# Expert blocks of a mixture-of-experts layer: two biases move from TensorE to VectorE

## The reference, cut to what matters

```python
logits = jnp.einsum('bsd,de->bse', input, Wg)          # E = 8 experts
top_vals, top_idx = jax.lax.top_k(softmax(logits), 2)  # two experts a token
h = relu(jnp.einsum('ebsd,edh->ebsh', xm, W1) + b1)    # 256 -> 512
y = jnp.einsum('ebsh,ehd->ebsd', h, W2) + b2           # 512 -> 256
out = jnp.sum(y * scores, axis=0)
```

## Time and profile before

| | |
|---|---|
| median of three runs | 1959.32 us |
| profiled execution, its own time | 1960.84 us |
| its span, first to last instruction | 1959.1 us |
| PE busy | 1750.1 us (89%) |
| DVE busy | 1140.5 us (58%) |
| ACT busy | 865.6 us (44%) |
| POOL busy | 1264.1 us (65%) |
| self-attention / cross-attention / experts (from the timeline) | to 217 / to 1698 / to 1959.1 us |

### The profile page before, as it was taken

How to read it: one execution, slowest core, us unless ns; L and a number is a source line. 1 busy time by engine, 2 the same in 40 slices (tenths; PEclk the granted TensorE clock), 3 DMA queues, 4 the chain that set the end, 5 groups by cost and what they waited for, 6 DMA issues and landing times. The chain is left out here.

```text
span 1959.1 us, 32737 instructions
## 1 busy us (share of the span) xinstructions
PE 1750.1 (89%) x10682; PEld 1225.8 (63%) x10682; DVE 1140.5 (58%) x2004; ACT 865.6 (44%) x1280; POOL 1264.1 (65%) x710
## 2 busy tenths in 40 slices
PE   6654799999989999998999999989999999648992
PEld 4544566676656666665666666656666665337991
DVE  4776455656565656656565656666665555563444
ACT  3223244444444544444444444544444444424443
POOL 3877247667677677686866766777668676236554
PEclk8776689999999999999999999999999999759996
DMA  6001300000200000010000000200000000032224
GB/s 193 1 22 34 117 1 23 1 22 0 77 1 23 22 2 23 0 55 22 22 1 24 1 22 0 77 1 23 22 1 23 16 0 1 33 123 77 70 71 140
DMA packets 38853, 68.09 MB, mean 35 GB/s; under 512 B 4600, under 2 KB 28544, under 8 KB 37696
## 3 DMA queue, kind: packets, MB, share of 16 engines
q1 hardware_dynamic: 34976, 56.12, 8.6%
q0 software_dynamic: 3744, 10.23, 1.7%
HBM read 52.84 MB, written 13.50 MB: 34 GB/s over the span
## 5 line engine op out<-in xcount | busy, mean ns | idle before, releaser
L1101 POOL TENSOR_TENSOR xa_total<-xa_total,xa_pexp 128x1024 f32<-128x1024 f32 (+1 forms) x341 | 832.3, 2441 | 62.0 <-ACT xa_pexp L1042 38.1
L1174 DVE TENSOR_REDUCE xa_parts<-ps_ring 128x1 f32<-128x402 f32 x1024 | 531.6, 566 | 269.8 <-PE ps_ring L987 256.4
L1042 ACT ACTIVATE xa_pexp<-ps_s 128x1024 f32<-128x1024 f32 (+1 forms) x416 | 426.5, 1027 | 397.6 <-PE ps_s L941 360.9
L955 PE MATMUL ps_pv<-xa_pexp,xa_v 128*64 128x512 f32 (+1 forms) x1664 | 398.7, 603 | 0.0
L955 PEld LDWEIGHTS ps_pv<-xa_pexp,xa_v 128*64 128x64 f32 (+1 forms) x1664 | 106.0, 136 | 182.1 <-issue 141.1
L941 PE MATMUL ps_s<-xa_q_neg,xa_row_one 64*128 64x512 f32 (+1 forms) x832 | 180.2, 391 | 0.0
L1101 POOL TENSOR_TENSOR xa_total<-xa_pexp 128x1024 f32<-128x1024 f32 x31 | 74.0, 2387 | 159.9 <-ACT xa_pexp L1042 158.6
L1077 ACT COPY xa_v<-ps_ring 128x256 f32<-128x256 f32 (+1 forms) x208 | 77.7, 374 | 204.1 <-PE ps_ring L926 202.2
L987 PE MATMUL ps_ring<-xa_k_hi,xa_q_hi 64*128 64x402 f32 x512 | 127.0, 377 | 6.0 <-DVE xa_parts L1174 5.0
L987 PE MATMUL ps_ring<-first_k_hi,xa_q_hi 64*128 64x402 f32 x512 | 123.8, 388 | 3.3 <-DVE xa_q_lo L1168 1.5
L1189 DVE RECIPROCAL xa_inv<-xa_sums 128x128 f32<-128x128 f32 x128 | 120.3, 942 | 2.9 <-ACT xa_sums L1064 2.7
(11 more groups left out here) (298 smaller groups left out, 3434.9 us busy)
## 6 DMA issues: line engine op xcount, KB each, us to landing
wa_raw<-in_pack_a SPq DMA_DIRECT2D x17, 768.0 KB, 4.5
ex_raw<-in_pack_e SPq DMA_DIRECT2D x8, 1024.0 KB, 5.9
ctx_raw<-in_ctxT SPq DMA_DIRECT2D x4, 1601.0 KB, 8.8
wb_raw<-in_pack_b SPq DMA_DIRECT2D x16, 256.0 KB, 2.7
ex_w_hi<-ybuf SPq DMA_DIRECT2D x8, 512.0 KB, 7.4
sa_xT<-in_xT SPq DMA_DIRECT2D x8, 256.0 KB, 6.3
X<-in_x SPq DMA_DIRECT2D x1, 2048.0 KB, 11.3
x_hi<-sa_x1s_hi SPq DMA_DIRECT2D x16, 128.0 KB, 2.1
```

The lines of the kernel that those rows point to most:

```text
L955: ins = nc.tensor.matmul(ps_pv[half(h), :], v[0:m, t, at:at + XD], pexp[0:m, buf, h, :], start=t == 0, stop=t == MT - 1)
L1042: nc.scalar.activation(pexp[0:m, buf], ps_s[0:m, (p * MT + t) % 2], ACT.Exp, scale=XD ** -0.5)\
L1101: engine.tensor_tensor(total[p][0:m], first, pexp[0:m, buf], ALU.add).then_inc(s["add_done"], 1)
L1174: nc.vector.tensor_reduce(parts[:, h, q, c:c + 1], ps_ring[:, r, 0:CW], AX.X, ALU.max)\
```

## The change

Both bias products leave PE. b1 and b2 are held as fp32 tables on all 128 partitions, and DVE adds the block's row while it moves h and y out of PSUM; the row is picked by a register that DVE loads itself. b2's table is loaded from DRAM by broadcast; b1, which lies turned in DRAM, is turned on PE at the start of the stage, copied to SBUF by DVE, stored to DRAM by SP and loaded again by broadcast; these stand ahead of the stores of `x2` in SP's list. ACT's `sel`, its copy of h and `bx` go. To make room (the tables take 24 KB a partition), xb, h_f, h_hi and h_lo have one buffer instead of two, the one-hot table `one_r` has half the size and is used in turn, and the routing's small tiles share their place with the block loop's. The second layer starts at the high part of h and waits for the low part only before its last four products. Cut to its core:

```diff
@@ Ahead.start
-        sp.dma_start(self.b2_raw[:], a["b2"]).then_inc(self.sems["small_in"], 16)
@@ experts, tiles
-        bx = sb("bx", [P, HID + E], F32R)
+        b1_all, b2_all = sb("b1_all", [P, NE, HID]), sb("b2_all", [P, NE, E])
-        xb_hi, xb_lo = sb("xb_hi", [P, 2, E], F32R), sb("xb_lo", [P, 2, E], F32R)
-        sel = sb("sel", [P, 2, P], F32R)
+        xb_hi, xb_lo = sb("xb_hi", [P, E], F32R), sb("xb_lo", [P, E], F32R)
+        h_f, h_hi, h_lo = sb("h_f", [P, HID]), sb("h_hi", [P, HID], F32R), sb("h_lo", [P, HID], F32R)
@@ sync
+            sp.dma_start(b2_all[:].rearrange("p e n -> p (e n)"),
+                         a["b2"].rearrange("(o e) n -> o (e n)", o=1).broadcast_to([P, NE * E])).then_inc(s["b2_in"], 16)
+            sp.wait_ge(s["b1_turned"], 1)
+            sp.dma_start(ahead.b1_rows.rearrange("o (e n) -> (o e) n", e=NE), b1_row[:]).then_inc(s["b1_out"], 16)
+            sp.wait_ge(s["b1_out"], 16)
+            sp.dma_start(b1_all[:].rearrange("p e n -> p (e n)"), ahead.b1_rows.broadcast_to([P, NE * HID]))\
+                .then_inc(s["b1_in"], 16)
             for b in range(B):
                 sp.wait_ge(s["x_done"], NC * (b + 1))
@@ tensor
+            for c in range(HC):
+                ins = nc.tensor.transpose(ps_y[0:NE, 1, c * P:(c + 1) * P], b1c[:, :, c], ident[:])
+            ins.then_inc(s["b1_tr"], 1)
...
-                pe.wait_ge(s["sel_done"], q + 1)
-                nc.tensor.matmul(ps_h[:, q % 2, :], sel[:, q % 2], bx[:, 0:HID], start=False, stop=True)\
...
             def second_layer(q):
                 e = experts_of[q]
-                pe.wait_ge(s["h_done"], q + 1)
+                pe.wait_ge(s["h_hi_done"], q + 1)
                 need(pe, s["y_copied"], q - 1)
-                nc.tensor.matmul(ps_y[:, q % 2, 0:E], sel[:, q % 2], bx[:, HID:HID + E], start=True, stop=False)
...
+                    if n == 2 * HC:
+                        pe.wait_ge(s["h_done"], q + 1)
@@ scalar
             def take_x(q):
                 act.wait_ge(s["xb_tr"], q + 1)
-                need(act, s["h_mm"], q - 1)
+                need(act, s["h_mm"], q)
-                nc.scalar.copy(sel[:, q % 2], pick[:, q:q + 1].bitcast(F32).broadcast_to([P, P])).then_inc(s["sel_done"], 1)
-            def take_h(q):
...
             for q in range(NBK):
-                take_h(q)
                 if q + 1 < NBK:
                     take_x(q + 1)
@@ vector
             for b in range(B):
                 statistics(NC * b, s["var_ready"])
+            dve.wait_ge(s["b1_tr"], 1)
+            nc.vector.tensor_copy(b1_row[:], ps_y[0:NE, 1, :]).then_inc(s["b1_turned"], 1)
...
-            nc.vector.tensor_scalar(second[:], row_of[:], float(LO), -float(LO), ALU.is_ge, ALU.mult)
-            nc.vector.tensor_tensor(row_of[:], row_of[:], second[:], ALU.add)
...
             for n in range(0, ASG, 8):
+                if n >= 16:
+                    dve.wait_ge(s["table_step"], n // 8 - 1)
...
-            nc.vector.tensor_copy(eidi[:], eid[:])
-            nc.vector.tensor_tensor(pick[:], eid[:], row_of[:].broadcast_to([P, NBK]), ALU.is_equal)
+            link(nc.vector.tensor_copy(eidi[:], eid[:]))
...
-            dve.wait_ge(s["b_hi_done"], 2)
-            nc.vector.tensor_tensor(bx[LO:LO + NE, 0:HID], ...)
-            nc.vector.tensor_tensor(bx[LO:LO + NE, HID:HID + E], ...)
...
+            def take_h(q):
+                e = dve.value_load(eidi[0:1, q:q + 1], min_val=0, max_val=NE - 1)
+                experts_of[q] = e
+                dve.wait_ge(s["h_mm"], q + 1)
+                need(dve, s["h_tr"], q)
+                nc.vector.tensor_tensor(h_f[:], ps_h[:, q % 2],
+                                        b1_all[:, bass.ds(e, 1), :].rearrange("p a n -> p (a n)"), ALU.add)\
+                    .then_inc(s["h_copied"], 1)
             def take_y(q):
...
-                nc.vector.tensor_copy(y_sb[:, q % 3], ps_y[:, q % 2, 0:E]).then_inc(s["y_copied"], 1)
+                nc.vector.tensor_tensor(y_sb[:, q % 3], ps_y[:, q % 2, 0:E],
+                                        b2_all[:, bass.ds(experts_of[q], 1), :].rearrange("p a n -> p (a n)"), ALU.add)\
+                    .then_inc(s["y_copied"], 1)
+            dve.wait_ge(s["b1_in"], 16)
             take_x(0)
             for q in range(NBK):
+                take_h(q)
                 if q + 1 < NBK:
                     take_x(q + 1)
```

More of the change, by code:

```diff
@@ L797, in __init__ @@
         self.raw = [sb(f"raw{u}", [P, WW]) for u in range(STG)]
-        self.b1c, self.wg, self.b2_raw = sb("b1c", [P, NE, HC]), sb("wg", [P, EC, NE]), sb("b2_raw", [NE, E])
+        self.b1c, self.wg = sb("b1c", [P, NE, HC]), sb("wg", [P, EC, NE])
+        self.b1_rows = nc.dram_tensor("b1_rows", [1, NE * HID], F32, kind="Internal").ap()
         self.sems = sems(ctx, nc, "raw_in0 raw_in1 small_in")
@@ L1250, in experts @@
-        probs = sb("probs", [P, T, NE])
-        gred = sb("gred", [P, T])
-        top = sb("top", [P, T, 8])
-        idx = sb("idx", [P, T, 8], U32)
-        idxf = sb("idxf", [P, T, 8])
-        norm = sb("norm", [P, T, TOPK])
-        hot = sb("hot", [P, TOPK, T, NE])
-        mask = sb("mask", [P, T, NE])
-        below = sb("below", [P, P])
-        run = sb("run", [P, NE, T])
-        tot = sb("tot", [P, NE, T])
-        before_e = sb("before_e", [P, NE])
-        count = sb("count", [P, NE])
@@ L1264, in experts @@
-        steps16 = sb("steps16", [P, NE, T])
-        blocks, ends = sb("blocks", [P, NE]), sb("ends", [P, NE])
-        place = sb("place", [P, T, NE])
-        picked = sb("picked", [P, TOPK, T, NE])
-        pos, quo, rem = sb("pos", [P, ASG]), sb("quo", [P, ASG]), sb("rem", [P, ASG])
-        iota = sb("iota", [P, P])
-        iota_a = sb("iota_a", [P, ASG])
-        col = sb("col", [P, 1])
-        row_of, second = sb("row_of", [P, 1]), sb("second", [P, 1])
-        spare = sb("spare", [P, NBK])
@@ L1289, in experts, with tmp @@
-        h_hi, h_lo = sb("h_hi", [P, 2, HID], F32R), sb("h_lo", [P, 2, HID], F32R)
-        h_f, y_sb = sb("h_f", [P, 2, HID]), sb("y_sb", [P, 3, E])
+        norm = sb("norm", [P, T, TOPK])
+        gidx, sidx = sb("gidx", [P, NBK], U32), sb("sidx", [P, NBK], U32)
+        eidi = sb("eidi", [P, NBK], U32)
+        with ExitStack() as short:
+            def tmp(name, shape, dt=F32):
+                return short.enter_context(nc.sbuf_tensor("ex_" + name, shape, dt))
+            probs = tmp("probs", [P, T, NE])
+            gred = tmp("gred", [P, T])
+            top = tmp("top", [P, T, 8])
+            idx = tmp("idx", [P, T, 8], U32)
+            idxf = tmp("idxf", [P, T, 8])
+            hot = tmp("hot", [P, TOPK, T, NE])
+            mask = tmp("mask", [P, T, NE])
+            below = tmp("below", [P, P])
+            run = tmp("run", [P, NE, T])
+            tot = tmp("tot", [P, NE, T])
+            before_e = tmp("before_e", [P, NE])
+            count = tmp("count", [P, NE])
+            steps16 = tmp("steps16", [P, NE, T])
+            blocks, ends = tmp("blocks", [P, NE]), tmp("ends", [P, NE])
+            place = tmp("place", [P, T, NE])
+            picked = tmp("picked", [P, TOPK, T, NE])
+            pos, quo, rem = tmp("pos", [P, ASG]), tmp("quo", [P, ASG]), tmp("rem", [P, ASG])
+            iota = tmp("iota", [P, P])
+            iota_a = tmp("iota_a", [P, ASG])
+            col = tmp("col", [P, 1])
+            spare = tmp("spare", [P, NBK])
+            full, wrap, pad = tmp("full", [P, NBK]), tmp("wrap", [P, NBK]), tmp("pad", [P, NBK])
+            eid = tmp("eid", [P, NBK])
+            one_r = tmp("one_r", [P, ASG // 2, P], BF16)
+            with ExitStack() as late:
+                past = late.enter_context(nc.sbuf_tensor("ex_past", [P, NBK, NE], F32))
+            one_q = tmp("one_q", [P, ASG, NBK], BF16)
+            with ExitStack() as gate_only:
+                xT_f = gate_only.enter_context(nc.sbuf_tensor("ex_xT_f", [P, 2, EC, P], F32))
+                b1_row = gate_only.enter_context(nc.sbuf_tensor("ex_b1_row", [NE, HID], F32))
+            val_q = tmp("val_q", [P, ASG, 2, NBK], BF16)
@@ L1457, in _ @@
                         pe.wait_ge(s["val_done"], 2)
-                ins = nc.tensor.matmul(ps_y[:, 0, 0:2 * NBK], one_r[:, n], val_q[:, n].rearrange("p a q -> p (a q)"),
+                ins = nc.tensor.matmul(ps_y[:, 0, 0:2 * NBK], one_r[:, n % 16], val_q[:, n].rearrange("p a q -> p (a q)"),
                                        start=n == 0, stop=n == ASG - 1)
-            ins.then_inc(s["table_mm"], 1)
-            for c in range(HC):
-                ins = nc.tensor.transpose(ps_y[0:NE, 1, c * P:(c + 1) * P], b1c[:, :, c], ident[:])
-            ins.then_inc(s["b1_tr"], 1)
+                if n % 8 == 7:
+                    ins.then_inc(s["table_step"], 1)
             def turn_x(q):
@@ L1523, in _ @@
         def _(act):
-            act.wait_ge(s["zero_set"], 1)
-            nc.scalar.copy(bx[:], zero[:, 0:1].broadcast_to([P, HID + E]))
             def take_weights(e):
```

74 lines of the change are left out of this document (26 added, 48 removed).

## The result

| | before | after |
|---|---|---|
| median | 1959.86 us (10 runs, 1956.71 to 1963.3) | 1954.99 us (10 runs, 1953.18 to 1955.95) |
| profiled span | 1959.1 us | 1953.2 us |

The ratio is 0.9974, 95% interval 0.9966 to 0.9983: faster by 0.26%, about 5 us. The forecast was a gain of 10.65 us, to 1948.7 us. The time lies inside the range and the sign was right, but over half of the gain is missing. All medians and ratios here are of fast executions; a slow one of 2436.63 us among those of experiment e7 is left out.

What follows compares the result with a forecast made beforehand. PE alone was taken to bound the block loop, with a serial chain ahead of it. Terms of -10.6, -0.7, +1.5, -0.2, +0.65, -0.94 and -0.35 gave -10.65 us: 1948.7 us from the median 1959.32, range 1944.3 to 1955.8.

Steps and rivals of the forecast that it cites:

- First gather: Ahead of the loop: the gather waits out DVE's low weights, so block 0's x is split later, +0.65 us.
- Tables' transfers: Start of the last stage: b1's table load delays expert 2's load and the routing chain, +1.5 us.
- the shorter routing: Ready list ahead of the loop: two tiny operations on `row_of` leave the chain, -0.2 us.
- Blocks 0 to 7: Blocks before the PE-bound part: bias products go and x's cast no longer waits behind ACT's copy, -1.29 us.
- Loop: PE-bound blocks: h and y bias products go, 3.81 to 3.46 us a block, -10.6 us.
- the register load: DVE's new load per block in the loop: about 0.30 us, hidden with almost half a microsecond left, so zero.
- Last block: End of the loop: eight products run while DVE makes the low part, only four remain behind it, -0.7 us.
- A: Rival: ACT's late relu at 1796.79 us, a stall, doesn't come back; -3.4 us, 1945.3 us; chance 0.14.
- B: Rival: b1's table broadcast ahead of the loop runs at half the rate; +6.0 us, 1954.7 us; chance 0.12.
- C: Rival: DVE's register load closes a loop longer than PE's; 14 us back, 1962.5 us; chance 0.09.
- D: Rival: the edit doesn't reach the bound, PE waits replace the biases; about 1959 us; chance 0.05.

Runs made afterwards that it cites:

- e7: Kernel before without VectorE's two subtractions for the low parts of the biases (left out of the result); 1963.55 us against 1959.24, ratio 1.0033.
- e1: Changed kernel with SyncE holding expert 5's weight load until the first gather has landed; 1944.72 us, ratio 0.9946 to the kernel before.
- e2: Changed kernel with VectorE's low weights of experts 3 and 4 moved behind its low part of block 0's rows; ratio 0.9952 to the kernel before.
- e3: Changed kernel with the load of b1's table queued behind expert 2's weight load; 1951.41 us, ratio 0.9966 to the kernel before.
- c1: Changed kernel run again unaltered as a control, on chip 10; ratio 0.9980 to the kernel before.
- e12: Kernel before without its two bias products per block, second layer's first eight products waiting for h's high part alone; 1944.44 us, ratio 0.9944.
- e4: Changed kernel without VectorE's register loads (wrong table rows, same additions), run three times; ratios 0.9955, 0.9953 and 0.9955 to the kernel before.
- e10: Changed kernel with TensorE's second layer again waiting for h's low part before its first product; ratio 0.9998 to the kernel before.
- c4: Changed kernel run again unaltered as a control, on chip 8; ratio 0.9968 to the kernel before.
- e1 again: The kernel of e1 run once more, on chip 2; 1954.31 us over 12 runs (control 1952.99), ratio 0.9977 to the kernel before.

## Why the prediction was right or wrong

**First gather: the step that failed.** The prediction put it as "the first gather waits them out and ends at list + 0.08 + 2.25 + 0.86 = + 3.2 ... Turn, cast and low x follow": +0.65. The end of the instruction was right, 1755.27, 3.5 us after the list's last operation began. Wrong was "Turn, cast and low x follow": it let the rows come as fast behind the instruction as before, 1.9 us to PE, where they took 5.0. I had moved DVE's low weights earlier and asked only what they do to POOL; I did not ask what their end releases, SyncE's load. Measured +4.24: e1 puts 3.0 of it on the load, e7 makes all of it out of the kernel before, e2 takes all of it away.

**Tables' transfers.** Forecast +1.5, or +1.3 with the shorter routing; measured 0.57 at the list. e3 shows the large transfer costs nothing in its place. The error helped the result by 0.7.

**Blocks 0 to 7.** Forecast -1.29, measured -0.50. The forecast took the clock as it was before, and here it was low for longer (0.77 granted for 0.95). Relus 0 and 1 are 5.21 us apart at a granted clock of 0.67. This isn't the longer wait's doing: c1, with the same wait, has 3.58 us at 1.00, and e2, with the short one, has 5.17. By the table, relu 6 comes 1.8 us later behind the first turn of rows than before (36.9 us for 35.1), and ScalarE's stop, 2.0 us with its input ready where it was 3.4, gives 1.4 back. So even the -0.50 is in part luck.

**Loop.** Forecast 3.46 us a block, and that is what the chain shows; e12 gives the term its full size. The changed kernel's own loop gave 9.0 of 10.6. The mis-sized term is the register load, which I priced at zero with half a microsecond to spare. By the row it takes 299 to 550 ns, median 304, as PE's does, and 0.19 us of register arithmetic follows, which I had left out; e4 puts 0.6 to 1.9 us on the two. In a short block of the profile after they run beside the low part of h (from 1822.93 to 1823.52 us, the low part to 1823.61), so 0.1 us is all that they may lengthen before the addition itself is late. How that reaches PE isn't shown: in the long blocks it is PE's own group that is stretched or DVE's addition that begins late for no wait shown. The Trainium skill's 1.3 us for a TENSOR_LOAD (Runtime: NRT & Kernel Launch, The ~15µs preamble/postamble breakdown) is told of registers loaded from HBM and doesn't hold for this one, from SBUF.

**Last block.** -0.7, and e10 undoes it: right.

**Rivals.** A, the stop that doesn't come back: it came back, and c4, the same kernel without it, shows that this isn't the edit's doing. B fell: expert 2's cast began at 1723.68 us, not after 1728. C: the register loads do cost, 0.6 to 1.9 us and not 14; a loop through DVE that closes later than PE in every block is not what the chain shows. D fell: the period is 3.46 us.

Open: what ScalarE's stop is, why it comes on some chips alone, what sets the moment at which the clock returns to full, and why the times of e1 again scatter.

## What to carry over

When an instruction moves earlier, follow its end as well as its beginning: here it freed a buffer, the freed buffer let a 1 MB load go, and a gather of the critical path stood behind it for 3 us. If a large transfer may wait and a small one may not, make the large one's issue wait for the small one's landing. Two lines brought the rows 3 us earlier both times; that this shortens the whole kernel is clear on one chip and not on the other. And a product taken from the bounding engine is worth its whole time only if the next chain (here relu, low part, second layer, 3.63 us for 3.46) is loosened with it: 4.4 us over 29 blocks without, 10.2 with. Last, two profiles of one kernel (after and c1) differed by 2.4 us at relu 6, mostly where the clock was low in one and full in the other, so read a gain from the step that the edit moves, here gather to first turn, and not from a later point.

## What the runs showed that was not expected

- PE had the rows of a 128-row gather 3.1 us after POOL began it with nothing in its way, 4.3 us with a stretched instruction, and 7.3 to 7.5 us with a 1 MB load issued a microsecond before its instruction ended.
- The same kernel ran in 1950.0 us on one chip and 1953.0 to 1955.0 on others, most of it, by the profiles, one stop of ScalarE of 2 to 3.6 us at the same instruction and the slower blocks behind it. With the same register loads and the same stop, the loop at 3.63 us a block (e10) had blocks of 3.63 to 3.66 alone; the one at 3.46 had blocks up to 3.77.
- Taking 1.1 us of VectorE's work out of the kernel before cost 4.3 us (1963.55 against 1959.24).
